# Decoder layer: the filters' head means move from a matmul of their own into the gate's first layer

## What is computed

```
short, long = fir(v, short_w), fir(v, long_w)      # (b, l, H=4, DV=64)
gate_in = concat([hs, short.mean(2), long.mean(2), delta.mean(2)], -1)   # 256 + 3*64
logits  = gelu(gate_in @ fg_w1.T + fg_b1) @ fg_w2.T + fg_b2
wgt     = softmax(logits / temp)  (with a floor)
o       = wgt0*short + wgt1*long + wgt2*delta + wgt3*v
```

## Time and profile before

| what | value |
|---|---|
| median of 3 runs | 1272.36 us (1266.75 to 1273.87) |
| profiled execution, span from the first to the last instruction | 1263.7 us (no separate total is given for it; the median of the runs is 8.7 us above the span) |
| busy: TensorE / weight load / VectorE / ScalarE / GpSimd | 1102.6 / 841.4 / 867.7 / 515.0 / 559.6 us |
| chain that ended last | TensorE 50%, VectorE 11%, GpSimd 6%, issue 5%, ScalarE 4% |
| one of the passes 2 to 6 | about 102 us |

### The profile page before, as it was taken

One profiled execution on the slowest core, in us unless ns is written; L12 is line 12 of the kernel. 1 busy time (PEld: TensorE's weight loads), 2 busy tenths in 40 slices (PEclk: granted clock), 3 DMA queues, 4 the chain that ended last, 5 costly groups with the idle time before them and its releaser, 6 DMA issues.

```text
span 1263.7 us, 22566 instructions
## 1 busy us (share of the span) xinstructions
PE 1102.6 (87%) x7730; PEld 841.4 (67%) x7730; DVE 867.7 (69%) x2268; ACT 515.0 (41%) x936; POOL 559.6 (44%) x995
## 2 busy tenths in 40 slices
PE   4988889698799899899899899989989989987892
PEld 2645558577567777677586686777767666856782
DVE  4888986854666866866876776676686674556477
ACT  4767754415123512521521442351351244744561
POOL 4233435256037526544734843762652224344452
PEclk9989999888899999999999999999999999989996
DMA  6543441431001501330250160130110263223488
GB/s 169 168 145 131 129 154 57 179 98 66 19 1 43 180 35 37 112 105 1 76 182 1 59 193 1 43 127 13 34 60 35 85 217 97 89 76 110 132 268 310
DMA packets 86783, 127.47 MB, mean 101 GB/s; under 512 B 28304, under 2 KB 62608, under 8 KB 84496
## 3 DMA queue, kind: packets, MB, share of 16 engines
q1 hardware_dynamic: 79472, 106.30, 26.3%
q0 software_dynamic: 7200, 19.74, 4.3%
HBM read 66.47 MB, written 59.55 MB: 100 GB/s over the span
## 4 chain that ended last, share of the span: by engine, by line
PE 50%; DVE 11%; POOL 6%; issue 5%; ACT 4%; another core or an unknown queue 1%; DMA 1%; SPq 1%; ACTq 0%; DVEq 0%; POOLq 0%
PE bank L674 7%; PE bank L579 5%; PE bank L559 4%; PE bank L727 3%; PE bank L506 2%; PE bank L886 2%; ACT arena L1053 2%; PE bank L737 2%; PE bank L546 2%; PE bank L777 2%; PE bank L569 2%; PE bank L645 2%; POOL orn L1420 2%; PE bank L654 2%; POOL arena L1405 2%
## 5 line engine op out<-in xcount | busy, mean ns | idle before, releaser
L958 ACT ACTIVATE arena<-bank 128x512 f32<-128x512 f32 (+1 forms) x326 | 171.3, 545 | 457.7 <-PE bank L569 142.7
L1533 DVE SCALAR_TENSOR_TENSOR arena<-arena,param 128x512 f32<-128x512 f32 x144 | 106.2, 751 | 23.5 <-ACT arena L981 20.0
L1467 POOL DMA_INDIRECT results<-arena x78 | 76.5, 981 | 100.9 <-DVE arena L2089 72.6
L1403 POOL TENSOR_TENSOR arena<-arena 128x126 f32<-128x126 f32 (+22 forms) x217 | 90.2, 415 | 37.3 <-DVE arena L1633 21.8
L1387 POOL COPY arena<-arena 32x128 f32<-32x128 f32 x128 | 51.6, 403 | 103.0 <-DVE arena L1623 97.1
L674 PEld LDWEIGHTS bank<-arena 128*128 128x128 f32 x768 | 92.2, 198 | 7.1 <-issue 6.9
L1405 POOL TENSOR_TENSOR arena<-arena 128x126 f32<-128x126 f32 (+22 forms) x217 | 86.9, 400 | 17.0
L674 PE MATMUL bank<-arena 128*128 128x128 f32 x768 | 93.1, 282 | 0.0
L886 PE MATMUL bank<-arena 128*128 128x128 f32 x624 | 87.4, 286 | 1.1 <-ACT arena L1216 0.7
L1339 POOL DMA_INDIRECT slots_x<-arena x64 | 63.5, 992 | 49.2 <-DVE arena L1828 31.9
L886 PEld LDWEIGHTS bank<-arena 128*128 128x128 f32 x624 | 80.3, 201 | 2.5 <-issue 2.4
(11 more groups left out here) (269 smaller groups left out, 2682.0 us busy)
## 6 DMA issues: line engine op xcount, KB each, us to landing
arena<-slots_x SPq DMA_DIRECT2D x78, 129.0 KB
slots_x<-rows_of_no_token SPq DMA_DIRECT2D x8, 1161.0 KB
xt<-x_in SPq DMA_DIRECT2D x16, 512.0 KB, 4.7
kq_T<-kq SPq DMA_DIRECT2D x8, 1024.0 KB, 3.8
kq<-kq_T SPq DMA_DIRECT2D x8, 1024.0 KB
arena<-results SPq DMA_DIRECT2D x32, 256.0 KB
arena<-ffn_in SPq DMA_DIRECT2D x7, 768.0 KB, 4.1
vT<-v_T SPq DMA_DIRECT2D x8, 514.0 KB
```

The source lines that it names most:

```text
L958: free(act.activation(out_, in_, func, **kw), name)
L1403: own.link(pool.tensor_tensor(tmp, rows32[:, m0:, k].unsqueeze(2).broadcast_to([P, nm, k]), units[:, 0:k, k].unsqueeze(1).broadcast_to([P, ...
L1467: pool.indirect_dma_start(results[:, :], bass.IndirectOffsetOnAxis(ap=dest[:, n % YS:n % YS + 1], axis=0), ys[:, n % YS, :], None).then_in ...
L1533: ins = V.scalar_tensor_tensor(cv[:, k % 4, :], pre[:, j, d:d + GT], param[:, at + d:at + d + 1], cv[:, k % 4, :], ALU.mult, ALU.add)
```

## The change

The bank gm and its evacuation go. GpSimd adds the two channel halves of `sht` into `short_sum` and of `lng` into `long_sum` ([128, 512] each: head 0 + head 2 above head 1 + head 3). The gate's first layer takes these two as inputs, with weights in which the 64 rows of the filter's part of `fg_w1` stand twice, scaled by 1/4 at the start; so it has five matmuls for each output half instead of four. The rows are loaded twice, with four small transfers; the `long` weights take the place of `mean_s` and `mean_l` in the constant table, which are no longer loaded. The four dmT matmuls become two transpositions of 128x128 (two tiles' blocks side by side), so even tiles land on partitions 0 to 63 and odd ones on 64 to 127, and ScalarE evacuates with two instructions of 64x256. The order of the gate matmuls moves by one.

```diff
-        N_TABLES = 3
+        N_TABLES = 4
+        N_WEIGHTS = 4 + 4
...
-                    if m == 0 and k == 2:
-                        drained(pe, f"gm.{i}")
-                    rhs = (hsT[:, 0, :], hsT[:, 1, :], gmT[:, :], dmT[:, :])[k]
-                    last = mm(o[:, :], wgt("fg1", k, D)[:, m * P:(m + 1) * P], rhs, start=k == 0, stop=k == 3)
-                    if k == 3:
+                    if m == 0 and 2 <= k < 4:
+                        pe.wait_ge(sem("heads_summed"), 2 * i + k - 1)
+                    rhs = (hsT[:, 0, :], hsT[:, 1, :], short_sum, long_sum, dmT[:, :])[k]
+                    w_ = (wgt("fg1", 0, D), wgt("fg1", 1, D), short_w, long_w, wgt("fg1", 3, D))[k]
+                    last = mm(o[:, :], w_[:, m * P:(m + 1) * P], rhs, start=k == 0, stop=k == 4)
+                    if k == 4:
                         full(last, n)
 
-                n = f"gm.{i}"
-                o = open_bank(pe, n, next(body_bank))
-                pe.wait_ge(sem("short_done"), 2 * i + 2)
-                pe.wait_ge(sem("long_loaded"), 16 * (i + 1))
-                for k in range(4):
-                    src = (sht, lng)[k // 2]
-                    last = mm(o[:, :], cst(("mean_s", "mean_l")[k // 2]), src[:, k % 2, :], start=k == 0, stop=k == 3)
-                full(last, n)
                 if x and ahead:
                     front_gram(i + 1, 1)
                 pe.wait_ge(sem("hs_loaded"), 16 * (i + 1))
                 gate_hidden(0, 0)
+                gate_hidden(0, 1)
...
-                        gate_hidden(0, 1 + t)
+                        gate_hidden(0, 2 + t)
...
-                for t in range(T):
-                    last = mm(o[0:DH, t * P:(t + 1) * P], dm[:, t, :], ident, start=True, stop=True)
+                for k in range(2):
+                    last = tr(o[:, k * P:(k + 1) * P], dm[:, 2 * k:2 * k + 2, :].rearrange("p t d -> p (t d)"), ident)
                 full(last, n)
                 gate_hidden(1, 1)
+                gate_hidden(1, 2)
                 drained(pe, f"dmT.{i}")
-                gate_hidden(0, 3)
-                for k in range(2, 4):
+                gate_hidden(0, 4)
+                for k in range(3, 5):
                     gate_hidden(1, k)
...
-                evac(dmT[0:DH, :], o[0:DH, :], n, scale=1.0 / H)
+                dmt = dmT[0:DH, :].rearrange("p (k r t) -> p k r t", k=2, r=2)
+                for r in range(2):
+                    last = act.activation(dmt[:, :, r, :], o[DH * r:DH * r + DH, 0:2 * P]
+                                          .rearrange("p (k t) -> p k t", k=2), ACT.Copy, scale=1.0 / H)
+                free(last, n)
...
+            def head_sums(i):
+
+                for t in range(T):
+                    drained(pool, f"solve{t}{NQ - 1}.{i}")
+                pool.wait_ge(sem("short_done"), 2 * i + 2)
+                done(pool.tensor_tensor(short_sum, sht[:, 0, :], sht[:, 1, :], ALU.add), "heads_summed")
+                pool.wait_ge(sem("long_loaded"), 16 * (i + 1))
+                done(pool.tensor_tensor(long_sum, lng[:, 0, :], lng[:, 1, :], ALU.add), "heads_summed")
...
                 if i == 0:
                     front_solve(1)
                     front_cleared(1)
+                    head_sums(0)
                     front_steps(1)
                     front_rows(1)
                 elif ahead:
...
+                    head_sums(i)
                     front_solve(i + 1)
                     front_steps(i + 1, x, output_norm)
                 elif x is not None:
+                    head_sums(i)
                     norm_scale(1, "x", 2 * x + 2)
...
-                dve.wait_ge(w_loaded, 16 * 3)
+                dve.wait_ge(w_loaded, 16 * N_WEIGHTS)
...
+                for means in (short_w, long_w):
+                    once(V.tensor_scalar(means, means, 1.0 / H, None, ALU.mult))
...
-            sp.dma_start(const[:, LV0:], const_d[:, LV1:]).then_inc(tables_loaded, 16)
+            sp.dma_start(const[:, LV0:cst_at("mean_s")], const_d[:, LV1:HEADS0]).then_inc(tables_loaded, 16)
+            sp.dma_start(const[:, cst_at("ones"):], const_d[:, HEADS1:]).then_inc(tables_loaded, 16)
...
-            sp.dma_start(wt[:, FIRST_WEIGHTS:], weight_d[:, FIRST_WEIGHTS:]).then_inc(w_loaded, 16)
+            sp.dma_start(wt[:, FIRST_WEIGHTS:FILTERS], weight_d[:, FIRST_WEIGHTS:FILTERS]).then_inc(w_loaded, 16)
+            sp.dma_start(wt[:, FILTERS + D:], weight_d[:, FILTERS + D:]).then_inc(w_loaded, 16)
...
+            for k, dst in enumerate((short_w, long_w)):
+                for r in range(2):
+                    sp.dma_start(dst[DH * r:DH * r + DH, :], weight_d[DH * k:DH * k + DH, FILTERS:FILTERS + D])\
+                        .then_inc(w_loaded, 16)
```

More of the change, by code:

```diff
@@ L85 @@
     "gram_ready": 16, "diag_ready": 16, "units_ready": 1, "solved": 1, "diag_cleared": 4, "rows_ready": 8,
-    "compact_ready": 1, "blocks_ready": 1, "short_done": 2, "delta_ready": 4, "exp_ready": 1, "gate_ready": 2,
+    "compact_ready": 1, "blocks_ready": 1, "short_done": 2, "heads_summed": 2, "delta_ready": 4, "exp_ready": 1, "gate_ready": 2,
     "mix_ready": 2, "osq_ready": 2, "oms_ready": 2, "orms_ready": 2, "on_ready": 1,
@@ L137, in wgt @@
             return wt[:, a:a + width]
+        HEADS0, HEADS1 = CONST["mean_s"][0], CONST["mean_l"][1]
+        FILTERS = WEIGHT["fg1"][0] + 2 * D
+        short_w = wt[:, FILTERS:FILTERS + D]
+        long_w = const[:, cst_at("mean_s"):cst_at("mean_s") + D]
         ident_b = sb("ident_b", [P, P], BF16)
@@ L308, in decoder @@
                   for i in range(NG - 2)] + [shared_w] * 2
-        gmT = gflat[:, 0:GT]
+        short_sum = gflat[:, 0:GT]
         dmT = gflat[:, GT:2 * GT]
         h1T = gflat[:, 2 * GT:4 * GT].rearrange("p (c t) -> p c t", c=CK)
+        long_sum = h1T[:, 1, :]
         MT = wt[:, 0:T * 2 * P].rearrange("p (t i c) -> p t i c", t=T, i=2)
@@ L377, in decoder @@
         ffn_loaded = sem("ffn_weights_loaded")
-        N_DVE_SETUP, N_POOL_SETUP, N_MAIN_SETUP = 7, 14, 3
+        N_DVE_SETUP, N_POOL_SETUP, N_MAIN_SETUP = 9, 14, 3
         block = es.enter_context(nc.Block())
@@ L459, in _ @@
                 if i == 0:
-                    pe.wait_ge(w_loaded, 16 * 3)
+                    pe.wait_ge(w_loaded, 16 * N_WEIGHTS)
                 beta_logits(i)
@@ L1124, in body @@
                         probs(1)
-                n = f"gm.{i}"
-                o = filled(act, n)
-                evac(gmT[:, :], o[:, :], n)
                 if x:
```

## The result

The changed kernel takes 1291.97 us (median of 4 runs, 1287.78 to 1296.31), the kernel before 1271.09 us beside it (4 runs): ratio 1.0181, 95% interval 1.0148 to 1.0214, slower by 20.9 us. Predicted was 1292.0 (1279 to 1300). The profiled execution took 1287.78 us; its span is 22.2 us longer than that of before.

A forecast was written before the change was run, and what follows sets the result against it. TensorE, busy 87%, was the engine to follow, but VectorE's bank release holds Gram 1. Start 1.3, pass 0 4.1, passes 1 to 6 -2.4 and pass 7 16.7 sum to +19.7 us on the median 1272.36: 1292 us (1279 to 1300).

The forecast's parts named there:

- Passes 1 to 6, the filter part: TensorE without gm: VectorE's bank release holds Gram 1, so 0.5 us of 2.7 us taken out arrives per pass.
- TensorE's saving arrives in full: Rival, 8%: VectorE not in the way between Grams 0 and 1; passes 1 to 6 give -16.1, total 1278.4 us.
- The state means: Two transpositions save 0.77 us, a fifth gate matmul adds 0.86; TensorE reaches the filter transpositions 0.1 us later.
- GpSimd's sums: Two two-input sums of 128x512, 1.15 us each, hidden in 5.96 us of GpSimd idle time in passes 1 to 6.
- the two simple bounds: For one GpSimd sum: 0.61 us (a two-input 128x256) below, twice that, 1.22 us, above.
- Pass 0: The sums stand ahead of GpSimd's substitution, which begins 4.77 us later; the gate's logits start 4.1 us later.
- Pass 7: Sums behind GpSimd's eight pad scatters; TensorE stands 17 us, out0 starts 14.5 later, clock 2.1, means 0.1: +16.7 us.
- partly made up in the tail: Rival, 10%: the expert phase has its own bound and takes up some of pass 7's stall; 1275 to 1287 us.
- pass 7 does not wait: Rival, 3%: GpSimd reaches pass 7's sums before 984.7, the saving holds in all passes; -13.4, 1259 us.
- the clock falls in every pass: Rival, 8%: TensorE's 2.5 us idle before Gram 1 lowers the clock, 6 x 2.1 us added; 1304.6 us.
- The start: More small loads, landing 0.3 us late, and VectorE scaling two more 128x256 blocks (0.73 us): +1.3 us (0.7 to 2.8).

The follow-up runs named there:

- e3: As e2, with gate matmuls (0, 0) and (0, 1) ahead of the next pass's Gram 1 on TensorE; ratio 0.9946 to the kernel before.
- e6: As e3, with each of GpSimd's two sums made twice in passes 1 to 6; ratio 0.9934 to the kernel before.
- e2: As e1, with VectorE instead of GpSimd making the two sums of pass 0; ratio 1.0014 to the kernel before.
- e1: The changed kernel with pass 7's sums ahead of the pad scatters on GpSimd; ratio 1.0036 to the kernel before.
- e9: The kernel before, TensorE's gate matmul (0, 1) of pass 7 waiting for a GpSimd write of 128x8 behind the pad scatters; ratio 1.0133.
- e8: As e7, with gate matmuls (1, 0) and (1, 1) ahead of out1 in pass 7; ratio 0.9914 to the kernel before.
- e10: The changed kernel, unaltered, in 6 more runs and one more profile; ratio 1.0159 to the kernel before, 1288.51 us.
- e7: As e3, with gate matmul (0, 2) ahead of the third Gram and the fourth Gram behind out0; ratio 0.9939 to the kernel before.
- e11: The kernel of e8, unaltered, run again beside the changed kernel; ratio 0.9928 to the kernel before, 1260.92 us against 1270.58.
- e4: The kernel before with only the dmT part of the change (two transpositions, two evacuations of 64x256); ratio 0.9976.
- e5: The kernel before, gate matmul (0, 1) of pass 7 waiting for a bare GpSimd semaphore increment behind the pad scatters; ratio 1.0046.

## Why the prediction was right, and where its sizes were off

The time (1292.0 against 1291.97) and the mechanisms were right. That the two agree so closely is luck: 19.7 us were forecast on top of 1272.36, and 20.9 (18.8 to 27.2) were measured on top of 1271.09, and the terms were off in both directions. Against the profiled span, one profile of each kernel:

| step | predicted | measured |
|---|---|---|
| start | +1.3 | +0.5 |
| pass 0 | +4.1 | +4.15 |
| passes 1 to 6, without the clock | -2.4 | -2.4 |
| passes 1 to 6, the clock | 0 | +3.0 |
| pass 7 | +16.7 | +15.9 |
| tail | 0 | +1.1 |
| sum | +19.7 | +22.2 |

The rows are read as shifts: 0.48 us when pass 0 starts (Gram 0 at 245.83 against 245.35), 4.63 when pass 1 starts, 4.27 at its mark. Passes 1 to 5 give 0.36, 0.34, 0.37, 0.54 and 0.56; pass 6 gave +2.74, which is +3.0 of clock less 0.26.

**Passes 1 to 6, the filter part.** Right in mechanism: Gram 1 starts with VectorE's release, and of TensorE's saving most became idle time, 2.48 us (predicted: about 2.5). e3 shows it from the other side: work put into that time brought 0.7 to 0.9 us a pass. The rival "TensorE's saving arrives in full" is refuted. The state means added 0.1 in the prediction; the end part took 4.53 us from dmT to the filters, as before, so they added nothing.

**GpSimd's sums.** 1.15 us taken, 1.27 measured, in all eight passes alike (1264 to 1272 ns for the first). It is a little over twice the half-size row of 0.61, so no start is saved: the upper of the two simple bounds, 1.22, was the better choice. The Trainium skill, GPSIMD Engine Reference, section 3.1, gives some 2.6 cycles an element for two inputs; at its 1.2 GHz that makes an estimate of 1.11 us for 512 elements. The trace has 1.27, and decides. The sums beside VectorE (pass 2) and those with VectorE idle (pass 7) take the same, but no instruction of VectorE with two SBUF inputs fell beside them, so the contention that the Trainium skill, GPSIMD Engine Reference, section 1, names was not tested on them. That the sums are hidden in passes 1 to 6 was shown by doubling them (e6).

**Pass 0.** Right in size and cause: e2, which takes only the sums away from GpSimd there, brings 3.8 us. The substitution was 5.2 us late, 0.4 more than predicted.

**Pass 7.** Right in mechanism, 0.8 us too much. The wait was 16.79 us (about 17 predicted), and out0 starts at 1008.73 instead of 988.31. Less the 5.20 us by which the pass began late, the gate matmul behind the wait came 14.2 us after its old place (14.5 predicted); what came behind it, the clock above all, made 1.7 instead of 2.2. e1 shows that the order on GpSimd makes it, e9 that a wait alone, of 13.07 us there, costs 14.2 to 19.4 us. The rival "partly made up in the tail" does not hold: SyncE's wait grew from 66.0 to 82.1 us. What the prediction did not see is that TensorE's saved time would meet a wait for VectorE there even without the stall (e1, e8). So "pass 7 does not wait" would have given what e1 shows, 1.0036 of the kernel before, about 1277 us, and not 1259: counting the passes' gain in full was the wrong price for that rival.

**The clock.** The rival "the clock falls in every pass" was neither right nor excluded: it falls in some. In the four profiles with the 2.48 us stretch (changed kernel, e10, e1, e2) it fell behind 5 of 24, for 3.0, 2.9, 1.5, 2.9 and 1.5 us (from pass distances, against passes of the same number without a fall). The stretches of 0.56 and 0.98 us (e3 and e6) and 0.56 us (e7, e8, e11) were followed by none in 30 passes. The term should have been, over six passes, about one fall of 2.4 us, with 0 to 6 us for the range.

**The start.** That the small loads would be late (0.3 us) was wrong: VectorE came to the scalings 1.28 us earlier than before and found them landed. The scaling itself takes 0.66 us (22.66 to 23.32; 0.73 taken). How these two became +0.48 by pass 0 was not tried, and one profile of each cannot tell it: the first Gram of pass 0 starts at 244.75 to 246.79 in the four profiles with the old start (before, e4, e5, e9) and at 245.01 to 247.39 in the nine with the new one. The averages, 245.8 and 246.3, are 0.5 apart too, but the predicted 1.3 is not excluded.

**The tail.** 1.1 us more in one profile and 3.4 in e10; not tried. The stretch behind the last mark, whose code is the same in all kernels, takes 233 to 237 us in e1 to e4 and 253 to 261 in e5 to e9 and e11, so neither number is more than the spread.

## What to carry to other kernels

Work that is moved to an engine with idle time must be placed by what stands ahead of it in each pass, first and last ones too: one call behind eight scatters, instead of ahead of them, cost 16 us, more than all of the 14.8 us of TensorE work that the change took out. Before removing work from the busiest engine, look for what ends its next wait; if another engine's release does, put other work in the gap by reordering, since that is where the gain came from (e3); in the 30 passes with the gap filled the clock did not fall. A mark that is to say that an engine has reached a point should be made by an operation of that engine, not by a bare semaphore increment behind DMA issues.

## What the hardware showed that was not expected

- The granted clock fell behind some of equal idle stretches and not behind others: 5 of 24 of 2.48 us (all five in passes 4 and 6), and in pass 7, behind 1.97 us, in e1, e2 and e7 but not in e3 and e6. What decides it is not known. Waits of 1.4 to 1.8 us of TensorE stand in passes 1 to 6 of every kernel here, and no fall followed one. The run-to-run spread goes with the clock in part: in e1's 12 runs the longest, 1260.75 us, has a mean clock of 0.952, the shortest, 1247.21, one of 0.964 (correlation -0.95). But e4, which has no such stretch, shows the same (-0.91), and e3 does not, so how much of the spread these falls make is not shown.
- A bare semaphore increment on GpSimd's queue behind eight indirect scatters went up at least 0.15 us before the first of them began (e5); a write of 128x8 waited for all eight (e9).
- A wait of 13.07 us made pass 7 14.0 us longer (e9). With one of 2.9 us the pass was 7.6 us longer (e5), but 2.67 us of this are a second wait, for a late semaphore of which no run shows the cause, and part is the clock; so e5 gives no price for a short wait.
